# Mixture of experts on one Trainium2 core: an expert for each half of a slot tile

## What is computed

```python
def _L0_ffn_ref(x, Wg, gamma, beta, W1, b1, W2, b2):   # 8 experts, top 2, 256 -> 1024 -> 256
    scores = xf @ Wg
    w, idx = jax.lax.top_k(scores, K)
    w = jax.nn.softmax(w, axis=-1)
    xhat = (xf - mu) * jax.lax.rsqrt(var + EPS)
    normed = xhat[None, :, :] * gamma[:, None, :] + beta[:, None, :]
    h = jax.nn.relu(jnp.einsum('end,edf->enf', normed, W1) + b1[:, None, :])
    out = jnp.einsum('enf,efd->end', h, W2) + b2[:, None, :] + xf[None, :, :]
    cw = jnp.sum(w[..., None] * jax.nn.one_hot(idx, E, dtype=w.dtype), axis=1)
    y = jnp.einsum('ne,end->nd', cw, out)
```

## Time and profile before

| | us |
|---|---|
| median of 3 runs | 2633.59 (2632.6 to 2636.88) |
| span of the profiled execution | 2633.5 |
| PE busy | 2184.0 (83%) |
| DVE busy | 1659.6 (63%) |
| ACT busy | 1208.2 (46%) |
| POOL busy | 598.8 (23%) |

### The profile page before, as it was taken

One profiled execution on the slowest core, in us unless ns is written; L12 is line 12 of the kernel. 1 busy time (PEld: TensorE's weight loads), 2 busy tenths in 40 slices (PEclk: granted clock), 3 DMA queues, 4 the chain that ended last, 5 costly groups with the idle time before them and its releaser, 6 DMA issues. The chain is left out here.

```text
span 2633.5 us, 42436 instructions
## 1 busy us (share of the span) xinstructions
PE 2184.0 (83%) x15678; PEld 1413.9 (54%) x15678; DVE 1659.6 (63%) x3371; ACT 1208.2 (46%) x2240; POOL 598.8 (23%) x543
## 2 busy tenths in 40 slices
PE   5996689897759995787799999996777898778787
PEld 3554247575449995343355555553555554555544
DVE  4875965466976665566756666626777534767653
ACT  2123855454533332422155556555565534566452
POOL 2210013134026663011211111003221223221041
PEclk8997789898869997888999999998998999898999
DMA  4111014343071113323322232102000001000000
GB/s 142 47 47 48 1 50 147 124 129 112 1 307 62 50 50 105 78 71 110 88 69 77 59 92 72 27 25 82 1 1 1 25 1 50 1 1 1 25 16 25
DMA packets 107451, 159.41 MB, mean 61 GB/s; under 512 B 26064, under 2 KB 85236, under 8 KB 104180
## 3 DMA queue, kind: packets, MB, share of 16 engines
q1 hardware_dynamic: 102836, 144.64, 17.8%
q0 software_dynamic: 4416, 12.06, 1.5%
HBM read 109.42 MB, written 47.19 MB: 59 GB/s over the span
## 5 line engine op out<-in xcount | busy, mean ns | idle before, releaser
L2874 DVE TENSOR_REDUCE xa_max<-psum 128x1 f32<-128x1024 f32 (+1 forms) x256 | 248.4, 988 | 137.7 <-PE psum L2784 137.0
L2955 ACT ACTIVATE xa_work<-psum 128x1024 f32<-128x1024 f32 (+1 forms) x208 | 212.6, 1023 | 180.1 <-PE psum L2807 178.9
L2822 PE MATMUL psum<-xa_work,xa_values 128*33 128x128 f32 (+1 forms) x3328 | 226.1, 279 | 0.0
L2822 PEld LDWEIGHTS psum<-xa_work,xa_values 128*33 128x33 f32 (+1 forms) x3328 | 169.3, 112 | 75.2 <-issue 71.3
L3200 PE MATMUL psum<-xa_c_parts,x_hl_f 128*128 128x512 bf16 x576 | 155.8, 420 | 61.3 <-ACT qk_raw_l L3408 24.6
L993 POOL TENSOR_TENSOR text_q<-text_q 128x512 bf16<-128x512 f32 x64 | 81.7, 1292 | 344.6 <-ACT text_q L1363 344.4
L1701 PE MATMUL psum<-moe_rows,moe_w 128*128 128x256 bf16 x1104 | 131.0, 276 | 5.6 <-issue 5.6
L2807 PE MATMUL psum<-xa_query_rows,xa_key_rows 98*128 98x512 bf16 (+1 forms) x416 | 128.5, 391 | 8.4 <-ACT xa_work L2955 7.7
L2784 PE MATMUL psum<-xa_key_rows,xa_query_rows 96*128 96x512 bf16 (+1 forms) x512 | 126.2, 342 | 8.6 <-ACT xa_work L2955 4.2
L3200 PEld LDWEIGHTS psum<-xa_c_parts,x_hl_f 128*128 128x128 bf16 x576 | 56.7, 105 | 137.3 <-issue 29.2
L1960 ACT CAST x_ch<-moe_raw 128x512 bf16<-128x512 f32 x92 | 56.9, 618 | 158.9 <-DVE moe_raw L1875 158.3
(11 more groups left out here) (482 smaller groups left out, 4822.1 us busy)
## 6 DMA issues: line engine op xcount, KB each, us to landing
text_q<-in_moe_w SPq DMA_DIRECT2D x64, 256.0 KB, 3.8
experts<-text_q SPq DMA_DIRECT2D x64, 256.0 KB, 3.1
moe_w<-experts SPq DMA_DIRECT2D x16, 1024.0 KB, 9.7
xa_key_rows<-cross_keys SPq DMA_DIRECT2D x48, 200.1 KB, 3.5
ctx_chunk<-in_ctxT SPq DMA_DIRECT2D x24, 300.0 KB, 3.0
cross_keys<-xa_k_hl SPq DMA_DIRECT2D x6, 800.5 KB, 3.8
moe_w<-pairs_out SPq DMA_DIRECT2D x8, 512.0 KB, 6.7
xa_ctx_f<-in_ctxT SPq DMA_DIRECT2D x4, 800.5 KB, 4.9
```

Source lines behind the costliest of these rows:

```text
L2822: ins = pe.matmul(total.ap[a * LANE:a * LANE + VC, c:c + PIECE], t["v"][b][0:rows, kt, first + a, :], exps[0:rows, a, c:c + PIECE], start= ...
L2874: v.tensor_reduce(t["maxes"][n % 2][:, qt * HU + a, part:part + 1], u.wide[:, 0:c1 - c0], AX.X, ALU.max).then_inc(*u.free)
L2955: act.activation(t["exps"][k % EXPS][0:rows], u.wide[0:rows].rearrange("p (m q) -> p m q", q=T), ACT.Exp, scale=1.0 / float(np.sqrt(np.flo ...
```

## The change

A half tile gets an expert of its own. An expert's pairs begin at a half tile of their own, so at most 32 + 7 = 39 half tiles hold pairs (`USED`), in 20 slots; the last slot has one. `owner_i` has an entry for each half tile. Matmuls of the first layer take the 128 rows of a half, with that half's weights; gamma, beta and both biases are addressed per half. PE loads the owner of each half in "turn" and once more in "second".

```diff
-SLOTS = PAIRS * NTOK // SLOT + NE - 1
+SLOTS = (PAIRS * NTOK // P + NE) // 2
 HALF_TILES = SLOTS * SLOT // P
+USED = PAIRS * NTOK // P + NE - 1
+def halves(j):
+    return range(min(2, USED - 2 * j))
...
PE:
-            owner[j] = pe.value_load(t["owner_i"][0:1, j:j + 1], min_val=0, max_val=NE - 1)
-            pe.wait_ge(*x_loaded(moved, j)(16 * 2 * (j // 2 + 1)))
+            for a in halves(j):
+                owner[j, a] = pe.value_load(t["owner_i"][0:1, 2 * j + a:2 * j + a + 1], min_val=0, max_val=NE - 1)
+            pe.wait_ge(*x_loaded(moved, j)(16 * (2 * (j // 2) + len(halves(j)))))
...
-                if j < NE:
-                    pe.wait_ge(*loaded(s, j)(32))
+                if 2 * j < NE:
+                    for e in (2 * j, 2 * j + 1):
+                        pe.wait_ge(*loaded(s, e)(32))
...
-                for h in range(HALVES):
-                    for k, (x, w) in enumerate(PASSES):
-                        ins = pe.matmul(u.ap[:, a * SLOT:(a + 1) * SLOT], w1[:, w, h, cf], t["x"][j % 2][:, x, h, :],
-                                        start=(h, k) == (0, 0), stop=(h, k) == (1, 2))
+                for i in halves(j):
+                    for h in range(HALVES):
+                        for k, (x, w) in enumerate(PASSES):
+                            w1 = t["w1"][:, :, w, h, cf][:, bass.ds(owner[j, i], 1), :].rearrange("p o f -> p (o f)")
+                            ins = pe.matmul(u.ap[:, a * SLOT + i * P:a * SLOT + (i + 1) * P], w1,
+                                            t["x"][j % 2][:, x, h, i * P:(i + 1) * P], start=(h, k) == (0, 0), stop=(h, k) == (1, 2))
...
-            for a in range(2):
+            for a in halves(j):
+                mine = pe.value_load(t["owner_i"][0:1, 2 * j + a:2 * j + a + 1], min_val=0, max_val=NE - 1)
...
-                        ins = pe.matmul(u.ap[:, a * D:(a + 1) * D], t["hidden"][j % 2][:, x, f, q], w2[:, w, f, :],
+                        w2 = t["w2"][:, :, w, f, :][:, bass.ds(mine, 1), :].rearrange("p o d -> p (o d)")
+                        ins = pe.matmul(u.ap[:, a * D:(a + 1) * D], t["hidden"][j % 2][:, x, f, q], w2,
...
DVE:
-            for a in range(2):
-                ins = v.tensor_scalar(t["act"][n % 2][:, a, :], u.ap[:, a * SLOT:(a + 1) * SLOT], bias[:, 2 * q + a:2 * q + a + 1],
-                                      0.0, ALU.add, ALU.max)
+            for i in halves(j):
+                bias = m.cols[:, b1:b1 + NE * 8].rearrange("p (e f) -> p e f", f=8)[:, bass.ds(owner[j, i], 1), :].rearrange("p o f -> p (o f)")
+                for a in range(2):
+                    ins = v.tensor_scalar(t["act"][n % 2][:, a, i * P:(i + 1) * P], u.ap[:, a * SLOT + i * P:a * SLOT + (i + 1) * P],
+                                          bias[:, 2 * q + a:2 * q + a + 1], 0.0, ALU.add, ALU.max)
...
ACT:
-            for h in range(HALVES):
-                ins = act.activation(t["value"][j % 2][:, h, :], u.ap[:, h * SLOT:(h + 1) * SLOT], ACT.Identity,
-                                     scale=column("moe_gamma", j, h), bias=column("moe_beta", j, h))
+            for a in halves(j):
+                for h in range(HALVES):
+                    ins = act.activation(t["value"][j % 2][:, h, a * P:(a + 1) * P], u.ap[:, h * SLOT + a * P:h * SLOT + (a + 1) * P],
+                                         ACT.Identity, scale=column("moe_gamma", j, a, h), bias=column("moe_beta", j, a, h))
```

More of the change, by code:

```diff
@@ L1558, in experts @@
                  top=sb("gate_top", [P, TILES]), gsum=sb("gate_sum", [P, TILES]), weight=sb("pair_weight", [P, PAIRS, TILES]),
-                 count=sb("tile_count", [P, NE]), base=sb("tile_base", [P, NE]), owner=sb("tile_owner", [P, SLOTS]),
-                 owner_i=sb("tile_owner_i", [P, SLOTS], INT), come=sb("come_from", [P, HALF_TILES], INT), go=sb("go_to", [P, HALF_TILES], INT),
+                 count=sb("tile_count", [P, NE]), base=sb("tile_base", [P, NE]), owner=sb("tile_owner", [P, HALF_TILES]),
+                 owner_i=sb("tile_owner_i", [P, HALF_TILES], INT), come=sb("come_from", [P, HALF_TILES], INT), go=sb("go_to", [P, HALF_TILES], INT),
                  minus=sb("minus_mean", [P, TILES]))
@@ L1576, in experts @@
         t["hot"] = short[:, 0:hots].bitcast(BF16).rearrange("p (i x c) -> p i x c", x=3, c=HALF_TILES)
-        at = hots
+        at = max(hots, PAIRS * TILES * NE * NE)
         for name, n in (("chosen", PAIRS * TILES * NE), ("place", TILES * NE), ("sc", TILES * NE), ("gate", TILES * NE),
-                        ("slot", PAIRS * TILES), ("high", PAIRS * TILES), ("spread", PAIRS * TILES * NE), ("got", HALF_TILES), ("row", HALF_TILES)):
+                        ("slot", PAIRS * TILES), ("high", PAIRS * TILES), ("spread", max(PAIRS * TILES, HALF_TILES) * NE), ("got", HALF_TILES), ("row", HALF_TILES)):
             t[name] = short[:, at:at + n]
@@ L1642, in experts_sp @@
     for j in range(SLOTS - 2, SLOTS):
[L1643 removed]
+        sp.wait_ge(*sent(moved, j)(16 * (2 * (j // 2) + len(halves(j)))))
     sp.wait_ge(*use["second", SLOTS - 1].full)
@@ L1705, in experts_pe @@
             u = use[step]
-            w2 = t["w2"][:, bass.ds(owner[j], 1), :, :, :].rearrange("p o x f d -> p (o x) f d")
             pe.wait_ge(*s.low_p(2 * (j + 1)))
@@ L1783, in experts_dve @@
     v.wait_ge(*s.v_step.now())
-    v.scalar_tensor_tensor(place, base[:].unsqueeze(1).to_broadcast([P, TILES, NE]), float(SLOT),
+    v.scalar_tensor_tensor(place, base[:].unsqueeze(1).to_broadcast([P, TILES, NE]), float(P),
                            u.ap[:, 0:TILES * NE].rearrange("p (t e) -> p t e", e=NE), ALU.mult, ALU.add).then_inc(*u.free)
@@ L1859, in experts_dve @@
         if kind == "turn":
-            owner[j] = v.value_load(t["owner_i"][0:1, j:j + 1], min_val=0, max_val=NE - 1)
+            for a in halves(j):
+                owner[j, a] = v.value_load(t["owner_i"][0:1, 2 * j + a:2 * j + a + 1], min_val=0, max_val=NE - 1)
             u = use[step]
@@ L1889, in experts_dve @@
             v.wait_ge(*u.full)
-            v.tensor_tensor(t["y_out"][j % 2], u.ap.rearrange("p (a d) -> p a d", d=D),
-                            t["b2"][:, bass.ds(owner[j], 1), :].to_broadcast([P, 2, D]), ALU.add).then_inc(*u.free)
+            for a in halves(j):
+                ins = v.tensor_tensor(t["y_out"][j % 2][:, a, :], u.ap[:, a * D:(a + 1) * D],
+                                      t["b2"][:, bass.ds(owner[j, a], 1), :].rearrange("p o d -> p (o d)"), ALU.add)
+            ins.then_inc(*u.free)
     v.wait_ge(*s.kept(TILES))
@@ L1939, in experts_act @@
     owner = {}
-    column = lambda name, j, h: m.cols[:, COL_AT[name][0]:COL_AT[name][0] + NE * HALVES].rearrange("p (e h) -> p e h", h=HALVES)[
-        :, bass.ds(owner[j], 1), h:h + 1].rearrange("p o h -> p (o h)")
+    column = lambda name, j, a, h: m.cols[:, COL_AT[name][0]:COL_AT[name][0] + NE * HALVES].rearrange("p (e h) -> p e h", h=HALVES)[
+        :, bass.ds(owner[j, a], 1), h:h + 1].rearrange("p o h -> p (o h)")
     for step in plan:
@@ L1944, in experts_act @@
         if kind == "turn":
-            owner[j] = act.value_load(t["owner_i"][0:1, j:j + 1], min_val=0, max_val=NE - 1)
+            for a in halves(j):
+                owner[j, a] = act.value_load(t["owner_i"][0:1, 2 * j + a:2 * j + a + 1], min_val=0, max_val=NE - 1)
             u = use[step]
```

14 lines of the change are left out of this document (6 added, 8 removed).

## The result

The changed kernel takes 2685.89 us (median of 4 runs, 2682.38 to 2688.53) against 2633.10 (4 runs, 2629.76 to 2636.88): 1.020 times the time, with a 95% interval of 1.018 to 1.021. I had said 2669 us, 2642 to 2700. The direction and the cause are those of A. The time is 17 us longer than A's sum; 12 of these lie in the stage of the experts, and one term explains them.

The account below looks back on a forecast made before the run. The array bounded the stage before; PE's instruction queue would after. Queue 284.7 plus semaphores 7.2, wait 2.0, ACT 0.5, end -1.5 gave 292.9 against 256.6 us: +36.3, so 2669 us, range 2642 to 2700.

Parts of the forecast that it names:

- A: Experts' stage: PE's instruction queue takes the array's place as bound; the forecast, 2645 to 2680 us, chance 0.76.
- 39x48 = 1,872 at 0.125: PE's queue, both layers: 48 fused register instructions for each of 39 halves, at 0.125 us each.
- The wait of slot 1: PE's wait for in_low of slot 1, 4.4 us on the queue before; 2.0 us kept for it.
- The array's demand: Experts' stage: 6.01 us per half, times 39 = 234 us, with short first-layer matmuls at 0.066 us each.
- B: Experts' stage: address work hides under the matmuls, so the kernel gets faster, 2615 us; chance 0.09.
- E: First layer: addresses hide, but register-addressed weight loads hold short matmuls 0.066 to 0.085 us apart; 2615 to 2650 us, chance 0.05.
- C: First layer: an address for each matmul, not each weight tile, 72 in place of 48 per half; 2786 us, chance 0.03.
- D: First layer: the array, idle a fifth of it, loses its clock; +43 us, 2712 us, chance 0.07.
- is used up and not rebuilt: PE's queue: its lead of 13 and 15 matmuls over the array goes, the queue being level in the second layer.
- DVE's bias instructions: DVE: 16 of 128 columns for 8 of 256, at 0.351 us, 5.6 for 3.5 us a slot; hidden.
- The end: Behind the loop: the last slot has one half, so one scatter in place of two and half an addition, -1.5 us.
- The experts' weights: DMA: weights now asked for two a slot, expected to land in time; nothing added.

Follow-up runs that it names:

- runs with pairs: Changed kernel with two weight-tile addresses worked out per register instruction, 936 in place of 1,872: 2614.06 us, 0.993 of before; run again, 2614.87 us.
- run with 256 columns: Changed kernel with the first layer 256 columns wide, both halves of a slot using the first half's expert: 2620.24 us.
- kept half: Paired-address kernel, one half's second layer reusing the owner register of the first layer: first half 2607.80 us (0.991 of before), second half 2617.63 (0.995).

## Why the prediction was right, and what was off

*A is shown.* The queue took the array's place: halving its register instructions takes 67 us off the stage, removing the first layer's takes 75 off, and 39 more loads add 26. Its lead over the array, 1.4 to 1.8 us before, is 0.10 us in most of the first layer.

*The mis-sized term* is "39x48 = 1,872 at 0.125". Count right, price too low: 1,872 x 0.132 = 247 us in place of 234. With 78 loads at 0.67 = 52 and 20 slots' semaphores at 0.34 = 7, the sum is 306 us, as measured; I had 292. Of the two rates in the earlier trace rows, each from 14 instructions, I kept near the lower, 0.123; 0.131 is near the mean of the 1,794 distances after, and stood as my upper bound (+11 us). A price that multiplies 1,872 wants its mean over the longest stretch that the trace offers.

*The wait of slot 1*, 2.0 us in the sum: PE waited 0.6 for POOL. The queue had fallen behind by then and met the semaphore late. So the stage is 11.7 us over my 293.9: 14 too little for the queue, 2 too much for the wait. Outside the stage I had 1 us less and the spans show no change; the other 3.6 of the 17 are the medians' growth of 52.8 against the spans' 49.2, which the spread of the runs covers.

*The array's demand* was too high in the sum for B: 0.066 us for a short matmul is 0.056, so the floor is 229 us, not 234. The row belonged to another stage; this didn't touch A, in which the array isn't asked.
By the Trainium skill, "TensorE: Matmul & The Clock Gate", section "Back-to-back issue gap", some 81 ns were to be expected for load and matmul with 128 columns; the runs with fixed and with paired addresses show 56, and the measurement decides. The changed kernel itself has 81, but there it is the queue's pace: alone it would have seemed to bear out the rival E.

*B* would have been right with addresses at 0.08 us: the runs with pairs are that case, 2614 us for B's 2615. That these agree so well is luck: B's floor is 5 us too high, and pairs still pay 9 us of stage for the queue. *C*: the count is 4 per block, not 6. *D*: the clock stayed at 1.00 from 900 to 1000 us with gaps of 1.2 us in each slot. *E*: short matmuls with addresses from a register (pairs) keep the same 0.056 as those with fixed ones. (E's upper end, 0.125 over 1.5, is 0.083 and not 0.085; nothing hangs on it.)

*The covers.* That the queue is level with the array in the second layer and its lead "is used up and not rebuilt" held for the sum; in the trace the lead grows from 0.1 to 0.6 us over each half, and the next load takes it. DVE's bias instructions are 0.344 long for my 0.351, but overlap: 87.9/312 = 0.28 us of busy time each, 4.5 us a slot for my 5.6. ACT's are 27.9/74 = 0.38 of busy time each, as I had them (0.386), though one lasts 0.457. Both are hidden. The end: from the stage's end to the last scatter's 2.2 us in place of 3.4, near the -1.5. The experts' weights delayed nothing.

*Open:* what makes one register instruction in eight come later; and which engine of the chain should be shortened to take the 1.0 us out of the slots in the run with 256 columns.

## What to carry to other kernels

Before splitting a matmul that is addressed through a register, count the register instructions and loads on PE's queue and set them against the array's time, stage by stage: narrower matmuls shorten the cover and lengthen the queue at once. Look for the count, not only for idle time: starved matmuls look busy. Where the queue is the bound, work out several addresses in one instruction, and put scalar loads where the queue has a lead, behind a row of long matmuls and not behind short ones and a wait.

## What the runs showed of the hardware

A register instruction of three operations took 0.046 us and started 0.124 us after the one before at best, 0.132 on average; one of six took 0.074 and the next started after 0.152 at best; one of two (kept half) 0.037 and 0.115. That is each time its own length and 0.078 us more, with 1.5 matmuls between as with 3. So three operations more cost 0.028, and an instruction less saves 0.078. A load of a scalar held PE's queue for 0.64 to 0.68 us on average; the stage paid for it where the queue had no lead. The queue ran at most some 18 matmuls ahead of the array: in the runs with pairs the lead stays level at 0.98 us over matmuls 0.056 us apart and, with one half's owner kept, at 1.94 us over those 0.109 us apart. Shorter matmuls therefore also make the cover shorter. Matmuls of 128 columns with their own weight load stood 0.056 us apart at the full clock, those of 256 columns 0.109.
